# Selective scan: delta*u*B from TensorE, by transposed du and a block-diagonal B

## The reference

```
x_dbl = einsum('bkdl,kcd->bkcl', xs, x_proj_weight)        # dts (6), B (16), C (16)
delta = softplus(einsum('bkrl,kdr->bkdl', dts, dt_projs_weight) + bias)
h[d, n] = h[d, n] * exp(delta[d, t] * A[d, n]) + (delta[d, t] * u[d, t]) * B[n, t]
y[d, t] = sum_n h[d, n] * C[n, t]    (+ D * u)
```

## Time and profile before

| | us |
|---|---|
| median of three runs | 15819.75 |
| the profiled execution | 15829.58, its span 15827.5 |
| DVE busy | 12523.3 (79%) |
| PE busy | 11783.6 (74%), weight loads 4298.9 (27%) |
| POOL busy | 10347.0 (65%) |
| ACT busy | 8208.0 (52%) |
| granted TensorE clock, mean | 0.769 |
| DMA | 484.53 MB, 523740 packets |

### The profile page before, as it was taken

The page is one execution under the profiler, slowest core; times in us unless marked ns, Lnnn a source line. Parts: engine busy times, 40 slices in busy tenths (PEclk is TensorE's granted clock), DMA queues, the critical chain, the costliest instruction groups (busy, mean ns, idle before and its releaser), DMA issues. The chain is left out here.

```text
span 15827.5 us, 206507 instructions
## 1 busy us (share of the span) xinstructions
PE 11783.6 (74%) x50304; PEld 4298.9 (27%) x50304; DVE 12523.3 (79%) x14967; ACT 8208.0 (52%) x15277; POOL 10347.0 (65%) x5876
## 2 busy tenths in 40 slices
PE   7777777777777777777777777777777777777777
PEld 2222422224222242222422224222242222422224
DVE  6999469994699946999469994699946999469994
ACT  4555455553555545555455553555544555455553
POOL 4888348883488834888358882588825888258882
PEclk8888688885887868888678875888868888688785
DMA  1111011110111101111011110111101111011110
GB/s 32 37 37 35 17 27 37 36 36 16 27 37 36 35 17 27 37 35 37 17 28 36 36 37 16 28 36 36 37 17 27 36 36 37 18 27 36 37 36 13
DMA packets 523740, 484.53 MB, mean 31 GB/s; under 512 B 160703, under 2 KB 457312, under 8 KB 523052
## 3 DMA queue, kind: packets, MB, share of 16 engines
q1 hardware_dynamic: 523052, 476.64, 14.1%
HBM read 27.61 MB, written 12.58 MB: 3 GB/s over the span
## 5 line engine op out<-in xcount | busy, mean ns | idle before, releaser
L499 POOL TENSOR_TENSOR arena<-arena 128x1024 f32<-128x1024 f32 x3072 | 7195.3, 2353 | 2074.1 <-PE ps L903 1937.6
L1172 DVE TENSOR_TENSOR_SCAN arena<-arena,ps 128x512 f32<-128x512 f32 x6144 | 7749.3, 1261 | 462.5 <-issue 443.5
L665 ACT ACTIVATE arena<-ps,negA 128x512 f32<-128x512 f32 x6144 | 4094.5, 683 | 3973.2 <-PE ps L864 3950.7
L861 PE MATMUL ps<-arena,spread 96*128 96x512 bf16 x6144 | 2854.7, 465 | 2616.0 <-DVE arena L1172 2551.7
L1141 DVE TENSOR_TENSOR ps<-ps,arena 128x512 f32<-128x512 f32 x6144 | 4148.7, 675 | 147.3 <-PE ps L861 119.0
L864 PE MATMUL ps<-arena,spread 96*128 96x512 bf16 x6144 | 2898.1, 472 | 500.0 <-ACT arena L665 499.7
L903 PE MATMUL ps<-arena,gather 128*32 128x256 f32 x24576 | 3186.0, 479 | 10.1 <-POOL arena L499 10.1
L861 PEld LDWEIGHTS ps<-arena,spread 96*128 96x128 bf16 x6144 | 622.5, 101 | 5802.4 <-DVE arena L1172 3362.6
L424 POOL TENSOR_TENSOR arena<-arena 128x512 f32<-128x512 f32 x512 | 649.3, 1268 | 1082.0 <-ACT arena L609 1077.4
L903 PEld LDWEIGHTS ps<-arena,gather 128*32 128x32 f32 x24576 | 685.4, 120 | 1945.5 <-issue 1883.8
L617 ACT ACTIVATE arena<-arena 128x512 bf16<-128x512 bf16 x768 | 478.9, 624 | 1034.9 <-POOL arena L463 1016.4
(11 more groups left out here) (178 smaller groups left out, 11266.6 us busy)
## 6 DMA issues: line engine op xcount, KB each, us to landing
arena<-arena SPq DMA_DIRECT2D x3072, 96.0 KB, 2.2
arena<-arena SPq DMA_DIRECT2D x512, 256.0 KB, 5.0
arena<-in_x SPq DMA_DIRECT2D x128, 192.0 KB, 3.2
out_tokens<-arena SPq DMA_DIRECT2D x64, 192.0 KB, 2.2
arena<-in_cw SPq DMA_DIRECT2D x1, 648.0 KB
xw_lo<-in_xbc_lo SPq DMA_DIRECT2D x1, 256.0 KB
xw_hi<-in_xbc_hi SPq DMA_DIRECT2D x1, 256.0 KB
arena<-in_spread SPq DMA_DIRECT2D x1, 192.0 KB
```

The lines of the kernel that those rows point to most:

```text
L499: pool.tensor_tensor(wgt[s % RW], hst[s % RH], c_rep[ch.par].unsqueeze(1).to_broadcast([P, 2, T]), ALU.mult).then_inc(weighted, 1)
L665: act.activation(decay[s % RDA][:, a, :], bank(3 + a), ACT.Exp, scale=negA[:, ch.k, group(s, a):group(s, a) + 1]).then_inc(decay_ready, 1)
L861: pe.matmul(bank(q % 3), spread[:, i, :], to_du[:, 2 * j + a, :], start=True, stop=True).then_inc(du_ready, 1)
L1172: dve.tensor_tensor_scan(hst[s % RH][:, a, flip], decay[s % RDA][:, a, flip], bank(q % 3)[:, flip], 0.0 if kind == 0 else state[:, q:q + 1 ...
```

## The change

`spread`, the bf16 parts and DVE's multiply go. The rows are laid out anew: a partition is one of 4 strips j times 32 channels, a step handles one group of 32 channels (NG = 6) and two states per strip, so a step covers 32 channels times 8 states, and 12 steps cover all. There are again 24 groups of 128x512 to scan.

- **du and B.** POOL makes du = delta*u in fp32. PE transposes it (`turn_du`) to tokens on partitions, 128 tokens at a time, those with t mod 4 = k; ACT saves it (`save_du`). PE transposes B (`turn_b`); ACT saves it (`save_bt`). SP writes B to DRAM in runs of 8 values so that reading with a shorter pitch gives, per token row, its 8 values of B at its own place among zeros: `b_diag`, 64 tokens x 64 tokens x 8 states per block. `fill` multiplies du (64 tokens x 32 channels) by it: the product is du*B for 64 tokens, 2 states and 32 channels.
- **The order in a tile.** For each half of 256 tokens, for each block k of four, for each strip j of four: sixteen matmuls of a half in one run, then the other half. The halves lie on partitions 0 to 63 and 64 to 127 of both operands. drive_ready is signalled once, after all 32.
- **delta.** DVE writes delta to `t_l`, SP writes it to DRAM and reads it four times (`load_delta`), replicated to the strips; ACT's decays read `delta_rep` in SBUF and not PSUM.
- **The scan** goes in halves of 256: four scans a step; the second half starts from the last column of the first.
- **C** goes through DRAM too. POOL multiplies `hst` in place, after `state_saved`; `hst` has eight buffers, `decay` three, and `wgt` goes.
- **Sums.** `gather` is 128x32, the matmuls are over 512 columns, in three batches of four steps, `SUM_SLOTS`.
- **Look-ahead.** `fill` and `decays` run two steps ahead, not one. The projection of the high channels and B, C comes first (v = 0), the low ones second; they have a bank each.
- **At the start** SP fills four DRAM tensors with zeros.

```diff
-    NSTEP = DI // GD // 2
-    NGRP = 2 * NSTEP
+NJ, CW = 4, P // 4
+NG = DI // CW
+NPR = NS // NJ // 2
+NSTEP = NPR * NG
+HALF, TB = T // 2, 64
+NB = HALF // TB
+RUN = NS // NPR
+PITCH = TB * RUN
+RING, RDA = 8, 3
...
+        SUM_SLOTS = {5: (0, 0), 6: (0, 1), 9: (1, 0), 10: (1, 1), NSTEP + 1: (2, 0), NSTEP + 2: (2, 1)}
+        GROUPS = (0, 1, 2, 3, 4, 5, 2, 3, 0, 1, 4, 5)
...
 SP
+                def prepare(ch):
+                    wait_apart(sp, bc_copied, ch.n(1, 1))
...
+                    sp.dma_start(c_dram[par], bc_raw[ch.d0 + NS:ch.d0 + 2 * NS, :]).then_inc(c_written, 16)
+                    wait_apart(sp, bt_saved, ch.n(1, 1))
+                    (four DMAs: b_t to runs in f_dram)
+                    wait_apart(sp, delta_done, ch.n(2, 1))
...
+                    sp.dma_start(delta_dram[par][DLO:DI, :], t_l[ch.r0:ch.r0 + DHI, :]).then_inc(delta_written[0], 16)
+                    load_b(0)
+                    load_c(0)
+                    wait_apart(sp, delta_done, ch.n(2, 2))
+                    sp.dma_start(delta_dram[par][0:DLO, :], t_l).then_inc(delta_written[1], 16)
+                    load_delta(0)
+                    load_delta(1)
+                    load_b(1)
+                    load_delta(2)
+                    load_c(1)
...
 POOL, a step
+                        pool.wait_ge(scan_done, ch.n(NSCAN, 4 * s + 4))
+                        if kind != 2:
+                            pool.wait_ge(state_saved, ch.saved(ch.c * NSTEP + (s + 1)))
...
+                        pool.tensor_tensor(h, h, c_rep[s // NG], ALU.mult).then_inc(weighted, 1)
+                        softplus_part(nx, 0) at s 2, times_u(nx, 0) at 3, softplus_part(nx, 1) at 5, times_u(nx, 1) at 7
...
 ACT, a step: save_state(s - 1), then
+                            if s == 1:
+                                copy_bc(nx)
+                                clamp_exp(nx, 0)
+                            if s == 2:
+                                save_bt(nx)
+                                square_log(nx, 0)
+                            if s == 4:
+                                clamp_exp(nx, 1)
+                            if s == 5:
+                                save_du(nx, 0)
+                                square_log(nx, 1)
+                            if s == 10:
+                                save_du(nx, 1)
+                        if s + 2 < NSTEP:
+                            decays(ch, s + 2)
...
 PE
+                def fill(ch, s):
+                    pr, g = s // NG, GROUPS[s]
+                    if s == 0:
+                        wait_apart(pe, dut_saved, ch.n(2, 2))
+                    if s % NG == 0:
+                        wait_apart(pe, b_loaded[pr], ch.n(32, 32))
+                    if not (ch.first and s < 2):
+                        wait_apart(pe, scan_done, ch.n(NSCAN, 4 * (s - 2) + 4))
+                    for h in range(2):
+                        rows = slice(h * TB, (h + 1) * TB)
+                        for k in range(NB):
+                            runs = b_diag[pr][:, k, :].rearrange("p (t j a) -> p j a t", j=NJ, a=2)
+                            for j in range(NJ):
+                                to = ps[j * CW:(j + 1) * CW, 2 * (s % 2) + h, :].rearrange("p (a t k) -> p a t k", a=2, k=NB)[:, :, :, k]
+                                mm = pe.matmul(to, du_t[ch.par][rows, k, g * CW:(g + 1) * CW], runs[rows, j, :, :], start=True, stop=True)
+                    mm.then_inc(drive_ready, 1)
...
 PE, a step: fill(s + 2), sums, then
+                            if s == 0:
+                                project(nx, 0)
+                            if s == 1:
+                                turn_b(nx)
+                            if s == 3:
+                                project(nx, 1)
+                            if s == 4:
+                                turn_du(nx, 0)
+                            if s == 9:
+                                turn_du(nx, 1)
+                        if s == 4:
+                            carry(ch)
...
 DVE, a step
+                        for i, half in enumerate(halves):
+                            cols = slice(half * HALF, (half + 1) * HALF)
+                            for a in range(2):
...
+                                dve.tensor_tensor_scan(h_out[:, a, cols][:, flip], decay[s % RDA][:, a, cols][:, flip],
+                                                       ps[:, 2 * (s % 2) + half, a * HALF:(a + 1) * HALF][:, flip],
+                                                       before, ALU.mult, ALU.add).then_inc(scan_done, 1)
+                        if nx:
+                            if s in (2, 6):
+                                at_least_log(nx, s // 6)
+                            if s in (3, 7):
+                                make_delta(nx, s // 7)
```

More of the change, by code:

```diff
@@ L491, in body @@
+                def pre(ch):
+                    for v in range(2):
+                        softplus_part(ch, v)
+                        times_u(ch, v)
                 def body(ch, nx, kind):
                     for s in range(NSTEP):
[L494 to L498 removed]
@@ L866, in pre, with project @@
-                def pre(ch):
-                    for z in range(2):
-                        project(ch, z, 0)
-                        project(ch, z, 1)
+                def project(ch, v):
+                    z = 1 - v
+                    if not ch.first:
+                        pe.wait_ge(dut_saved, ch.n(2, v - 1))
+                    if v == 1:
+                        pe.wait_ge(bt_saved, ch.n(1, 1))
+                    cols = bass.ds(ch.t0, T)
+                    pe.matmul(bank(HI_BANK + v), xw_lo[:, ch.k, z * P:(z + 1) * P], u_lo[:, ch.dir, cols], start=True, stop=False)
+                    pe.matmul(bank(HI_BANK + v), xw_hi[:, ch.k, z * P:(z + 1) * P], u_hi[:, cols], start=False, stop=True).then_inc(pre_filled, 1)
@@ new lines, in turn_b, with turn_du @@
+                def turn_b(ch):
+                    wait_apart(pe, bc_copied, ch.n(1, 1))
+                    if not ch.first:
+                        wait_apart(pe, dut_saved, ch.n(2, 0))
+                    r = slice(ch.d0, ch.d0 + NS)
+                    for k in range(NB):
+                        mm = pe.transpose(bank(LO_BANK)[:, k * NS:(k + 1) * NS], every(bc_raw[r, :], k), ident[r, ch.d0:ch.d0 + NS])
+                    mm.then_inc(b_turned, 1)
+                def turn_du(ch, v):
+                    wait_apart(pe, du_done, ch.n(2, v + 1))
+                    r = slice(0, P) if v else slice(ch.r0, ch.r0 + DHI)
+                    w = r.stop - r.start
+                    for k in range(NB):
+                        mm = pe.transpose(bank(HI_BANK + v)[:, k * w:(k + 1) * w], every(du[r, :], k), ident[r, r])
+                    mm.then_inc(du_turned, 1)
@@ new lines, in body @@
+                        if s in SUM_SLOTS:
+                            sum_states(ch, *SUM_SLOTS[s])
+                        if not ch.first and s + NSTEP in SUM_SLOTS:
+                            sum_states(before, *SUM_SLOTS[s + NSTEP])
+                        if nx:
[9 more added lines that the diff above has]
+                                turn_du(nx, 1)
```

542 lines of the change are left out of this document (210 added, 332 removed).

## The result

The changed kernel takes **17588.88 us** (median of 4 runs, 17585.18 to 17593.75); the kernel before, beside it, 15815.01 (4 runs, 15803.18 to 15823.9). The ratio is 1.1122, with a 95% interval of 1.1103 to 1.1142: 11% slower, where 14800 us were forecast. The profiled execution has a span of 17592.0 us, 1764.5 more than before.

The account below looks back on a forecast made before the run. VectorE was taken to set the pace, 47.3 us a chunk; after, 33.6 of work plus 9.4 idle is 43.0. From 15829.6, 256 chunks take 1101 off, 80 go on: 14809, median 14800 us, range 14300 to 15450.

Parts of the forecast that it names:

- The fill: On PE, 64 parts of 128 columns at 0.107 us, four strips at once, halves one after the other: 1.85 us.
- The rest of PE's sum: PE's sums, projections, carry and transposes beside the fills: 13.8 us a chunk at 2.4 GHz.
- rival A: Slower: strided parts in fill stream at half rate, PE becomes the bound; fill 3.5, chunk 58, 18650 us; chance 0.28.
- rival B: The fill's two halves overlap on different array rows: fill 0.95, chunk 39.0, 13780 us in all; chance 0.07.
- point of decision: The fill time from which PE, with its waits, reaches the 47.3 us a chunk of before: 2.5 us.
- the rule of the 16-byte line: Skill's rule against the forecast: an SBUF access needs two hits in a 16-byte line for full rate; no factor given.
- two cycles a column: Argument against slow strided parts: an fp32 part takes two cycles a column, so there may be room for a line each.
- Bounds of the fill: Fill on PE between 0.95 us if the halves overlap and 6.8 us if nothing does.
- The order's idle time: VectorE's waits a chunk from the step-by-step order of PE, ACT and POOL: 9.4 us idle.
- The DMA: Delta's way through DRAM to ACT's decays: there at 38.9, needed at 41.1, hidden with 2.2 us to spare.
- The clock: PE's clock in the scan stage, taken as 1.00 because PE streams 33 us of 43.
- A step of scans: Length of one of the 12 scan steps of a chunk on VectorE: 2.6 us.

Follow-up runs that it names:

- the flat kernels: Versions of the changed kernel with PE's loop over the six middle chunks written out; here e7_flat (17182 us) and e8_alt_flat (15603 us).
- e7_flat: Changed kernel with PE's loop over the six middle chunks of a direction written out, so no jump in the scan stage: 17182 us.
- e10_alt_pairs_flat: Changed kernel with the operand's columns read in pairs, the halves' matmuls in turn and PE's loop written out: 15234 us, 0.9633 of the kernel before.
- e8_alt_flat: Changed kernel with the two halves' matmuls in turn in fill and PE's loop written out: 15603 us, 0.9867 of the kernel before.
- after: The changed kernel itself, with no further edit, against the kernel before: 17589 us, ratio 1.1122.
- e6_pairs_flat: Changed kernel with the operand's columns read in pairs and PE's loop written out, each half's sixteen matmuls still in one run: 16229 us.
- e3_in: Changed kernel with fill's moving operand read from neighbouring columns (values then wrong, same work), output as it was: 16754 us.
- e9_alt_pairs: Changed kernel with the operand's columns read in pairs and the halves' matmuls in turn, PE's loop kept: 15903 us.

## Why the prediction was wrong

**The fill (failed, the main step).** The step was: "128 columns are 0.107 [...] fill = 1.85 us at 2.4 GHz". It measured 2.99. The 0.107 came from an operand without a step; for this one 0.232 from round to round was right, and 0.109 where the operand is contiguous. The rest of PE's sum held: 12 x 2.99 + 13.8 = 49.7 us a chunk, against 50.2 busy in the window. So this was rival A in kind: its price was a fill of 3.5 and 58 us a chunk, and the halves' overlap at the seam (rival B, in the small) brought that to 2.99 and 52.3 without the jump. The forecast had no overlap there ("two halves one after the other 1.71"); with a contiguous operand a fill took 1.56, so that by itself was too long by 0.3. Its point of decision, a fill of 2.5, is too high by the flat kernels at clock 0.99: 2.07 gives 46.14 a chunk, 2.99 gives 52.31, and a straight line between them crosses the 47.32 of before at 2.25. I held the rule of the 16-byte line against "two cycles a column", an argument of room that no row showed, and gave A 0.28. No row of before had such a step, and that was the reason to weigh the rule more.

**The jump (missing).** No step of the prediction spoke of it; e7_flat sizes it at 407 us. That is 23% of the 1774 us by which the kernel became slower.

**Bounds of the fill.** Bounds of 0.95 and 6.8 were right, and the lower one nearly reached: 1.19 with pairs and halves in turn (e10_alt_pairs_flat). Rival B had its mechanism right and the reason against it too ("the overlap can only be at the seam").

**The order's idle time (too small).** 9.4 us a chunk were forecast (its five terms add up to 9.5) beside 33.6 of VectorE's work. e8_alt_flat has nearly the fill and the clock that the forecast assumed (2.07 and 0.99), and no jump: there the three rows of VectorE stand 1649.5 + 1337.0 + 465.9 = 3452.4 us. Of these some 210 lie outside the eight scan stages, ahead of an image's first scan; inside them it is 12.7 us a chunk, and 46.14 stand where 43.0 were forecast. The wait of `at_least_log` is 4.9 there (forecast 4.4 for its first), that of `make_delta` 1.8 (3.1), and the scans' 6.0 (2.0 for fill(7) and the next chunk's first fill). The missing part is mostly the decays, 3.1, which I had taken to be always in time, and the sums that free the buffers of `hst`, 1.2, a wait that the step-by-step order does not have at all. In the changed kernel that wait was 6.6 us a chunk (1696.1 us). So even with the fill near the forecast, the gain would have been 15603 against 15821, 218 us, a fifth of the 1000 forecast.

**The miss by its parts.** A chunk took 53.96 us where 43.0 were forecast, 10.96 more. By the runs in a row (after, e7_flat, e8_alt_flat) the jump is 1.65 of it, the fill from 2.99 to 2.07 6.17, and what remains beside the forecast, mostly waits, 3.14.

**The DMA (nearly).** "Hidden with 2.2 to spare": the delta rows did make the decays wait, 327.8 us in e8_alt_flat, of which 242.3 inside the scan stages, 0.9 a chunk. In the changed kernel, with its longer chunks, it was 2.4 us in all stages together. They land, but not always in time for the next chunk's first decays.

**The clock.** 1.00 was taken, 0.98 measured in the stage. It was right for the wrong reason: PE was full because its parts were slow. With the short fills of e6_pairs_flat and e10_alt_pairs_flat it is 0.86 and 0.88.

**Right.** A step of scans (2.66 for 2.6), VectorE's work a chunk (46.14 - 12.67 = 33.5 for 33.6), and the time outside the stages (64.6 for 80).

**Open.** What of the 44.71 us in e10_alt_pairs_flat belongs to the clock and what to the order was not separated. The stall at the jump was shown by taking the jump away, and the fetch behind it by the packets in the pauses; why the fetch holds PE so much longer than the packet itself takes (1.2 us, median) stays open.

## What to carry over

When a matmul's moving operand is new, look first at how many bytes lie between two columns, and price it with a row that has that step; where none has, take the slow bound as a serious case, and see whether reading two neighbours in a row costs two lines of code. Small matmuls on different rows of the array should be issued in turn, since sixteen of a half in one run give half of the overlap away. And when an engine's instruction count goes up fourfold, look at its loops: count what stands between a jump and its target, and look at the instruction queue's bytes.

## What the runs showed of the hardware

- fp32 matmuls of 64 rows, 32 outputs and 128 columns: an operand with a step of 32 bytes between columns runs at 0.232 us a round of four strips, contiguous at 0.109; with pairs of columns or contiguous, a fill of 64 goes from 2.99 to 1.64 or 1.56. The step of 16 bytes in PSUM cost nothing (1.56 with and without it). With the step in the operand the fill took 3.03 at a granted clock of 0.50, hardly more than at 1.00.
- Halves in turn overlap whole: eight parts start where four did, every 0.232 us with the step and 0.115 with pairs. The fill goes from 2.99 to 2.07 and from 1.64 to 1.19, less than a factor of two, because four of the eight rounds of a half overlapped at the seam before.
- Without the step in the operand the granted clock was lower: 0.903 to 0.778 over the whole kernel when the fills were halved (e3_in), as PE's busy share went from 89% to 79%; with the step and halves in turn it stayed at 0.895, at a busy share of 80%. Of the 12 x 1.43 = 17.2 us of fill that e3_in takes off a chunk at full clock, 3.3 us came off the chunk.
- A jump back in PE's program over some 3350 matmuls and weight loads (two chunks) came with a pause of PE of 2.8 to 8.9 us (all jumps of after and e9_alt_pairs), of which 0.45 and 2.24 are there without a jump too; over some 650 (the kernel before) it cost nothing that could be measured.
- The packet behind such a pause: at 63 of the 64 jumps of the changed kernel a 16 KB packet of q8 runs in the pause, and PE starts 1.6 to 2.2 us after it has landed.
